# Scan layer: who multiplies the input by each row of B, and from which memory

## The reference, cut to what matters

```python
x_dbl = jnp.einsum('bld,ed->ble', x, x_proj_w)
delta_r = x_dbl[..., :DT_RANK]
B = x_dbl[..., DT_RANK:DT_RANK + D_STATE]
C = x_dbl[..., DT_RANK + D_STATE:]
delta = jnp.einsum('blr,dr->bld', delta_r, dt_proj_w) + dt_proj_b
delta = jax.nn.softplus(delta)
A = -jnp.exp(A_log)
dA = jnp.exp(delta[..., None] * A[None, None])
dBu = (delta * u)[..., None] * B[:, :, None, :]
def step(h, inp):
    dA_t, dBu_t, C_t = inp
    h = dA_t * h + dBu_t
    y_t = jnp.einsum('bdn,bn->bd', h, C_t)
    return (h, y_t)
```

## Time and profile before

| What | us |
|---|---|
| Median of 3 runs | 2095.08 (2091.97 to 2095.51) |
| Span of the profiled execution | 2109.5 |
| Scan layer in it, from its first transfer to the last addition to the stream | 586 to 788 |
| Its loop, first scan to last product with C | 629.5 to 778.8 |

### The profile page before, as it was taken

How to read it: one execution, slowest core, us unless ns; L and a number is a source line. 1 busy time by engine, 2 the same in 40 slices (tenths; PEclk the granted TensorE clock), 3 DMA queues, 4 the chain that set the end, 5 groups by cost and what they waited for, 6 DMA issues and landing times. The chain is left out here.

```text
span 2109.5 us, 32349 instructions
## 1 busy us (share of the span) xinstructions
PE 1714.7 (81%) x10854; PEld 1377.9 (65%) x10854; DVE 1329.9 (63%) x2578; ACT 912.2 (43%) x1761; POOL 705.7 (33%) x630
## 2 busy tenths in 40 slices
PE   6999788878845552835899999999999999999463
PEld 4434677667722222834788888888888888888353
DVE  3664644763469985445677667776777767774533
ACT  2456343333342322523455455554555545554232
POOL 3011333033357737034433223332333223330512
PEclk9899799879967885867899999999999999999676
DMA  3222332033200004430000000000000000000443
GB/s 79 49 37 79 113 120 84 31 120 108 88 7 0 0 3 157 138 112 3 8 6 9 11 11 2 10 10 10 10 10 7 10 10 2 10 6 6 133 136 107
DMA packets 79122, 97.67 MB, mean 46 GB/s; under 512 B 12064, under 2 KB 63776, under 8 KB 79024
## 3 DMA queue, kind: packets, MB, share of 16 engines
q1 hardware_dynamic: 72880, 79.59, 12.9%
q0 software_dynamic: 6144, 16.79, 2.5%
HBM read 62.25 MB, written 27.66 MB: 43 GB/s over the span
## 5 line engine op out<-in xcount | busy, mean ns | idle before, releaser
L1063 ACT ACTIVATE gqa_probs<-acc,gqa_bias,gqa_q_scale 128x128 f32<-128x128 f32 (+7 forms) x256 | 212.7, 831 | 258.8 <-DVE gqa_bias L1154 258.5
L1322 PE MATMUL aux<-gqa_probsT,gqa_v 128*128 128x128 f32 x2304 | 311.6, 282 | 1.4 <-ACT gqa_oT L1085 1.4
L1150 DVE TENSOR_REDUCE gqa_neg_max<-acc 128x1 f32<-128x128 f32 (+7 forms) x256 | 193.6, 756 | 165.8 <-PE acc L1289 163.3
L1322 PEld LDWEIGHTS aux<-gqa_probsT,gqa_v 128*128 128x128 f32 x2304 | 288.9, 198 | 8.2 <-issue 5.1
L1006 POOL TENSOR_TENSOR gqa_q_high<-gqa_straight,gqa_turned_q 128x512 fp32r<-128x512 f32 x64 | 81.5, 1274 | 510.9 <-DVE gqa_turned_q L1111 510.9
L1306 PE MATMUL aux<-ident,gqa_probs 128*128 128x128 f32 x1152 | 180.7, 280 | 7.6 <-DVE gqa_probsT L1182 4.6
L1342 PE MATMUL acc<-gqa_wo,gqa_oT 128*128 128x256 f32 x512 | 153.5, 427 | 4.8 <-DVE stream L1188 4.8
L1306 PEld LDWEIGHTS aux<-ident,gqa_probs 128*128 128x128 f32 x1152 | 135.9, 144 | 30.3 <-DVE gqa_probsT L1182 14.8
L1288 PE MATMUL acc<-gqa_k_high,gqa_q_high 128*128 128x512 f32 (+3 forms) x384 | 148.0, 385 | 1.0 <-ACT gqa_probs L1063 1.0
L1182 DVE COPY gqa_probsT<-aux 128x128 f32<-128x128 f32 (+3 forms) x256 | 123.0, 481 | 34.9 <-PE aux L1306 33.8
L1288 PE MATMUL acc<-gqa_k_high,gqa_q_low 128*128 128x512 f32 (+3 forms) x384 | 134.9, 351 | 0.0
(11 more groups left out here) (387 smaller groups left out, 4422.5 us busy)
## 6 DMA issues: line engine op xcount, KB each, us to landing
f_w<-in_f_up SPq DMA_DIRECT2D x64, 256.0 KB, 2.8
f_xs<-tokens_by_slot SPq DMA_DIRECT2D x108, 128.0 KB, 2.2
outputs_by_slot<-f_y_tile SPq DMA_DIRECT2D x108, 128.0 KB, 1.7
f_w<-in_f_down SPq DMA_DIRECT2D x64, 128.0 KB, 3.1
mat_qk<-mat_high SPq DMA_DIRECT2D x64, 64.0 KB, 2.3
gqa_w_q<-in_g_wq SPq DMA_DIRECT2D x32, 128.0 KB, 2.0
gqa_wo<-in_g_wo SPq DMA_DIRECT2D x32, 128.0 KB, 2.1
tokens_by_slot<-zeros SPq DMA_DIRECT2D x1, 3968.0 KB, 13.2
```

The lines of the kernel that those rows point to most:

```text
L1063: act.activation(probs[:, j % 4, 0:width(j)], scores(j), ACT.Exp, bias=bias[:, j % 16:j % 16 + 1], scale=q_scale[:, j // NT % 2, tile_of(j ...
L1150: dve.tensor_reduce(neg_max[:, j % 16:j % 16 + 1], scores(j), AX, ALU.max, negate=True).then_inc(max_ready, 1)
L1322: last = pe.matmul(aux[:, 2 + t // 4, t % 4 * P:(t % 4 + 1) * P], v[:, g, s, :], probsT[:, j % 4, s * P:(s + 1) * P], start=(s == 0), stop ...
```

## The change

DVE now makes `dbu` itself. It multiplies `du` (SBUF) by the spread row where PE left it, in banks 0 and 1 of `aux` (PSUM). POOL's 32 multiplications, ACT's 16 copies, the buffers `b_all` and the semaphore `b_ready` are gone. `spread_b(n)` now waits until DVE has made the products of step n-1, since they read its banks. DVE's list of stages is now `multiply`, `scan`, both of the same step.

```diff
--- before.py
+++ after.py
@@ -2105,7 +2105,6 @@
         z = sb("z", [P, DC, T])
         delta = sb("delta", [P, DC, T])
         du = sb("du", [P, DC, T])
-        b_all = sb("b_all", [P, 4, T])
         decay = sb("decay", [P, 4, T])
         dbu = sb("dbu", [P, 4, T])
         h = sb("h", [P, 4, T])
@@ -2129,7 +2128,6 @@
         du_ready = sem("du_ready")
         b_spread = sem("b_spread")
         c_spread = sem("c_spread")
-        b_ready = sem("b_ready")
         decay_ready = sem("decay_ready")
         dbu_ready = sem("dbu_ready")
         h_ready = sem("h_ready")
@@ -2164,17 +2162,6 @@
             for k in range(DC):
                 pool.wait_ge(delta_ready, k + 1)
                 pool.tensor_tensor(du[:, k], delta[:, k], core.xnT[:, k], ALU.mult).then_inc(du_ready, 1)
-            pool.wait_ge(du_ready, DC)
-
-            def multiply(i, j):
-                n = 4 * i + j
-                pool.wait_ge(b_ready, n + 1)
-                if not (start(i) and j < 2):
-                    pool.wait_ge(h_ready, 2 * n - 2)
-                for k in range(DC):
-                    pool.tensor_tensor(dbu[:, 2 * (j % 2) + k], du[:, k], b_all[:, j % 4], ALU.mult).then_inc(dbu_ready, 1)
-
-            pipeline(pool, STATE, [(0, multiply)], 4, lead=8)
 
         @block.scalar
         def _(act):
@@ -2197,13 +2184,6 @@
             act.wait_ge(delta_ready, DC)
             act.wait_ge(a_ready, 2)
 
-            def copy_b(i, j):
-                n = 4 * i + j
-                act.wait_ge(b_spread, n + 1)
-                if not (start(i) and j < 4):
-                    act.wait_ge(dbu_ready, 2 * n - 6)
-                act.activation(b_all[:, j % 4], aux[:, 0:2, :].rearrange("p a b -> p (a b)"), ACT.Copy).then_inc(b_ready, 1)
-
             def make_decay(i, j):
                 n = 4 * i + j
                 if not (start(i) and j < 2):
@@ -2212,7 +2192,7 @@
                     act.activation(decay[:, 2 * (j % 2) + k], delta[:, k], ACT.Exp,
                                    scale=a[:, k, bass.ds(n, 1)]).then_inc(decay_ready, 1)
 
-            pipeline(act, STATE, [(0, copy_b), (1, make_decay)], 4, lead=8)
+            pipeline(act, STATE, [(0, make_decay)], 4, lead=8)
 
         @block.vector
         def _(dve):
@@ -2239,6 +2219,17 @@
                 dve.wait_ge(relu_ready, k + 1)
                 dve.tensor_tensor(delta[:, k], delta[:, k], z[:, k], ALU.add).then_inc(delta_ready, 1)
 
+            dve.wait_ge(du_ready, DC)
+
+            def multiply(i, j):
+                n = 4 * i + j
+                dve.wait_ge(b_spread, n + 1)
+                if not (start(i) and j < 2):
+                    dve.wait_ge(h_ready, 2 * n - 2)
+                for k in range(DC):
+                    dve.tensor_tensor(dbu[:, 2 * (j % 2) + k], du[:, k], aux[:, 0:2, :].rearrange("p a b -> p (a b)"),
+                                      ALU.mult).then_inc(dbu_ready, 1)
+
             def scan(i, j):
                 n = 4 * i + j
                 c_all = aux[:, 2:4, :].rearrange("p a b -> p (a b)")
@@ -2257,7 +2248,7 @@
                     dve.wait_ge(h_ready, 2 * n + k + 1)
                     dve.tensor_tensor(hc[:, m], h[:, m], c_all, ALU.mult).then_inc(hc_ready, 1)
 
-            pipeline(dve, STATE, [(0, scan)], 4, lead=8)
+            pipeline(dve, STATE, [(0, multiply), (0, scan)], 4, lead=8)
             dve.wait_ge(summed, STATE * DC)
             for k in range(DC):
                 dve.scalar_tensor_tensor(z[:, k], core.xnT[:, k], channel[:, k, 1:2],
@@ -2300,7 +2291,7 @@
 
             def spread_b(i, j):
                 if not (start(i) and j < 1):
-                    pe.wait_ge(b_ready, 4 * i + j)
+                    pe.wait_ge(dbu_ready, 2 * (4 * i + j))
                 spread(0, 4 * i + j, b_spread)
 
             def spread_c(i, j):
```

## The result

| | us |
|---|---|
| Before, median of 20 runs | 2094.68 (2091.8 to 2098.02) |
| Changed, median of 20 runs | 2098.36 |
| Ratio | 1.0021, 95% interval 1.0014 to 1.0027 |

A forecast was written before the change was run, and what follows sets the result against it. DVE was taken to bound the scan layer's loop, its scans lengthened by POOL's products. Terms 42.3 + 0.9 - 35.8 + 2.4 = 9.8, counted as 9.65 us, took 2095.08 to 2085.4 us; range 2082.0 to 2089.5.

The forecast's parts named there:

- What bounded the loop: Scan layer's loop: DVE's work sets its length, scans taking turns with POOL's products; removing those gives back 42.3 us.
- The products at 1.12 us: DVE's 32 new products in the scan loop: 1.12 us each by their starts, adding 35.8 us.
- The start: Start of the scan loop: DVE's own product begins at about 627.1, filling 2.4 of 7.0 us of waiting.
- The added wait: PE's spread_b(n+1) waits for DVE's products of step n; claimed covered, PE's step 4.8 to 8.9 us against DVE's 8.87.
- I take no change: DVE's 3.49 us wait for PE's last sums behind the loop: taken as unchanged, between 1.0 less and 2.2 more.
- The barrier then moves all later layers ahead by the same amount, unchanged: Layers behind the scan layer: all start 9.65 us earlier and take the same time, giving 2085.4 us.
- Nothing else is priced: End of the added-wait step: no further cost counted, as every moved piece has cover.

The follow-up runs named there:

- e7: Kernel of e2 with 64 added POOL products of two SBUF inputs into a buffer nobody reads: 2147.86 us in its one run.
- e4: Changed kernel with 64 one-column memsets on DVE at the start of the scan layer: 0.9973 of before.
- e5: Changed kernel with DVE's scan-layer stages unrolled for 4 steps instead of 8, no filling: 0.9964 of before.
- e2: Changed kernel with 97 one-column memsets on DVE at the start of the scan layer: 2086.02 us, 0.9966 of before.
- e13: Changed kernel with 128 memsets on DVE, a shift of 159 instructions against before: grouped attention 1045.5 us in its one run.
- e12: Changed kernel, but POOL makes the k = 1 product from ACT's copy, PE spreads the next row before its sums, 108 memsets added: 2073.6 us, 0.9894 of before.
- e9: Kernel before with 16 memsets on DVE, a shift of 16 instructions: grouped attention 1059.0 us in its one run.
- e1: Kernel before with 31 one-column memsets on DVE at the start of the scan layer: 1.0062 of before.
- e11: Changed kernel with 12 memsets on DVE, a shift of 43 instructions against before: grouped attention 1051.0 us in its one run.

## Why the prediction was wrong

Right, by its own steps:

- **What bounded the loop**: DVE, with half of each long scan spent in turn with POOL's product. Forecast 42.3 us back; the scans' busy time fell from 113.5 to 71.3, 42.2 us. e7 shows the mechanism alone.
- **The products at 1.12 us**: DVE's step is 8.89 us against 8.87 forecast. The price of the Trainium skill (VectorE: DVE Perf Modes, section on the TRN2 errata), 1.19 us as an estimate, is near what a record lasts, 1.207. It is not what a product costs here, since the next instruction starts earlier.
- **The start**: the first product after 4.57 us of waiting, forecast near 4.7.
- **The added wait**: DVE never waited for a spread, as argued. Its only waits from 600 us to the layer's end are the 4.6 at the start, the 5.4 for the last sums and 1.5 for the transposes.

Off in size: **"I take no change" for the tail.** The last sums met the lower clock and cost 1.9 us, within the bound of 2.2. The transposes lost 1.1 more, which had no term. e4 shows the other side. So the layer gained 6.5 us instead of 9.65.

Wrong was the step **"The barrier then moves all later layers ahead by the same amount, unchanged"**, with "Nothing else is priced". It took a barrier to mean that untouched code behind it takes an untouched time. But the change also made DVE's code 31 instructions longer, and that moved a loop of 300 instructions, a thousand us of the program, to a place where it is fetched anew in each pass: 1.9 us a pass. With a packet of 128 instructions, the loop touches four packets there and three at the old place. Neither a rival nor a bound of mine had it, and the range of 2082.0 to 2089.5 ended below the result. e5 and e2 measured 2087.6 and 2086.0 with the same scan layer and a lucky place, inside the range, and gained 8.1 and 7.0 us on the kernel before in their series. What the forecast priced was that kernel.

The rows for it were at hand: the page lists the queues of instruction fetches, and the built program shows how many instructions each engine gains. What the trace of before could not show is that another place would be slow; only the length of the loop, 44 above two packets, could have hinted at odds of 43 in 128, and the packet's 128 instructions was shown only by e13.

## What to carry to other kernels

After an edit, count the instructions that it adds or removes on each engine ahead of any long hardware loop, also in layers that it doesn't touch, and compare the instruction-fetch queue and the waits without a releaser of the two profiles before blaming the edit; then move the code by some tens of instructions before giving the edit up. And look at the spread of a group's durations, not at its mean: two engines that take turns show as a second, twice as long kind of the same instruction, and work can be placed where they don't meet (e12).

## What was not expected of the hardware

- A loop of 300 DVE instructions costs some 2 us a pass at a slow place (120.4 to 120.5 us where fast places have 118.1 to 118.5) and 4 in e9 (122.8 us). It has five fetches a pass there and none at a fast place; the layer has 38 or 39 instead of 12 or 13. **Open**: why a pass costs more at a shift of 16 with as many fetches.
- The granted clock moves this layer too. Ahead of the first start of line 1144 it took 231.6 to 231.9 us in twelve of the sixteen profiles, and 235.0 to 236.7 in e1, e7, e11 and e12. DVE falls behind there in steps of 1.3 to 1.8 us, in stretches where the clock is 0.91 to 0.93 instead of 1.00. That is the surplus of e1 and e11 in the table, and of e7 and e12 (1037.5 us each) at a fast place. **Open**: why the clock fell in these four and not in the others, and what the profiled execution of before lost in its first two mixtures.
- A scan of 128x1024 in float32 takes 2.27 us against 1.20 for a product of the same size, twice as much even undisturbed.
- A DVE memset of one column takes 22 ns in a row of them (97 in 2.13 us), so that filling costs nothing where DVE waits.
